# Two of a head pair's 32 row maxima taken by ScalarE and GpSimd, twelve value segments in place of thirteen, and the reciprocal of the row sums on VectorE

## The chip, the cores and the metric

The kernel runs on 1 core of one Trainium2 chip. The metric is the device time of one execution in microseconds (us), lower being better. A change of 0.2% is about 4.8 us here.

## The reference

One transformer layer with attention and a mixture of experts side by side, all in float32: x is 8 x 1024 x 256, 16 heads of 16, 8 experts of width 352 of which each token takes 2, and a shared expert of width 704.

```python
xn = _layernorm(x)
# attention, per batch row b and head h
Q, K, V = xn @ Wq + bq, xn @ Wk + bk, xn @ Wv + bv
scores = einsum('bqhd,bkhd->bhqk', Q, K) * 16 ** -0.5 + alibi
attn   = softmax(scores, axis=-1)                 # row max, exp, row sum
out    = einsum('bhqk,bkhd->bqhd', attn, V) @ Wo + bo
# experts
top_logits, idx = top_k(xf @ Wg, 2); probs = softmax(top_logits)
y = sum over the token's 2 experts of prob * (silu(xf@W1[e]) * (xf@W2[e])) @ W3[e]
y = y + (silu(xf@Ws1) * (xf@Ws2)) @ Ws3
return x + out + y
```

## The kernel before

One program order (`Order.run`) is walked by five classes (Tensor, Vector, Scalar, Pool, Sync), each of which issues its engine's part; `Turn.wait_ge` adds semaphore waits. So every engine executes in the order written there, and nothing reorders it.

The stages are: layer norm and projections (to about 200 us), attention (to about 1415 us), the 71 blocks of the routed experts (to about 1890 us), and the shared expert with the output projection.

Attention works on **pairs** of heads, 64 in all (`NPAIR`). For a pair r there are two passes over the 1024 x 1024 scores of each head:

- The **max pass** (`max_unit`, 32 units a pair): a matmul of 128 queries by 512 keys into one PSUM bank of a ring of four (banks 4 to 7), then VectorE reduces it to a row maximum in `mx`. A "double" (half-units 2k and 2k+1 where k stands in `DOUBLE`) is one reduction over two banks. After a pair's last unit `fold` (VectorE) takes the maximum of the two halves into `m16`, GpSimd negates it and splits it in high and low parts (`mneg`), VectorE transposes it (`max_rows`, `mT`), and SyncE sends it through HBM (`Md`) into rows 52 and 53 of the query operand (`place_rows`), so that the score matmul subtracts the maximum.
- The **score pass** (`scores`, 32 a pair): a matmul of 128 keys by 512 queries into a ring of three banks (0 to 2), then ScalarE's exp into one of eight `pt` buffers (`pta`, `ptb`). `values` multiplies those with V into bank 3, in four column groups at once; V holds 16 ones beside each head, so rows of bank 3 are the row sums.

The max pass runs ahead: when the score pass of pair r begins, the max pass stands at unit 24 of pair r+1.

`PAIR` writes the order out by hand, one string for two key chunks: `S` one score, `u` one max unit, `P` one value segment, `T` the transpose of the next pair's maxima. `WIDTHS` gives the columns of each `P`; a pair has 4096 of them (8 chunks of 512), and the segments run two chunks behind the scores. When a pair's last column is done ScalarE copies bank 3 to `accs`. `heads(r, i)` then turns the sums over: SyncE fetches them as 128 x 16 (`sq`), GpSimd raises them to the power -1 (i = 1), SyncE sends them out and back in broadcast (`Sd`, `asum`), GpSimd multiplies `accs` by them (i = 3), and SyncE stores the result.

Beside attention GpSimd also issues DMAs (clearing slots, packing expert weights, scattering rows, loading V), and in pairs 0 to 18 the routing (`route`, tiles `r_...`) runs in small steps on VectorE and GpSimd, two steps a pair.

In the profile the matmul line L569 is a helper's: all matmuls but the transposes have it. `ps<-OPS` with 54 or 52 rows are scores and max units, `ps<-pta,VB` and `ps<-ptb,VB` are value segments. L1054 is a double, L1051 a single reduction, L1064 the fold, L1070 the transpose, L889 the exp, L897 the copy of bank 3, L1314 to L1319 the negation, L1326 the power -1, L1330 the multiplication by it, L1581 and L1575 the two DMAs of the maxima.

## Time and profile before

| | us |
|---|---|
| time, median of 3 runs (2382.97 to 2386.32) | 2384.82 |
| span of the profiled execution, first to last instruction | 2353.9 |
| VectorE busy in the span | 1978.7 (84%) |
| TensorE busy | 2316.8 (98%) |
| ScalarE busy | 1709.7 (73%) |
| GpSimd busy | 1012.1 (43%) |

The profile gives no time of the profiled execution beyond its span; the median of the timed runs lies 30.9 us above it, which is start and end around the instructions. Shares of the whole span mix stages; in the slices of the page VectorE reads 9 (90% or more) in attention and 5 to 7 afterwards. TensorE's busy time is modelled at its matmuls' ends and pipelined, so 98% doesn't say that it has nothing to give. The granted TensorE clock was full in all 40 slices.

### The profile page before, as it was taken

How to read it: one execution, taken by the hardware profiler on the slowest of the kernel's cores; microseconds unless marked ns; L12 is line 12 of the kernel's file. 1: busy time of each engine (PE TensorE's matmuls, PEld its weight loads, DVE VectorE, ACT ScalarE, POOL GpSimd, SP SyncE). 2: the span in 40 equal slices, each digit the busy share in tenths (PEclk: the TensorE clock that was granted, in tenths of full speed). 3: DMA queues.
4: the chain of work that ended last, by engine and by line, in shares of the span. 5: the costliest groups of instructions: out<-in, count | busy, mean ns of one | idle time of the engine just before them, and what ended most of it. 6: DMA issues, size and time to landing. Idle time of an engine off the chain costs nothing.

```text
span 2353.9 us, 50539 instructions
## 1 busy us (share of the span) xinstructions
PE 2316.8 (98%) x19358; PEld 1543.2 (66%) x19358; DVE 1978.7 (84%) x2874; ACT 1709.7 (73%) x3276; POOL 1012.1 (43%) x1013
## 2 busy tenths in 40 slices
PE   7999999999999999999999999999999999999998
PEld 6875444444444444444444438999999989888998
DVE  7888999999999999999999966777777765555555
ACT  4447888888999999998999997777777753333332
POOL 2112556553225555454454334434343354455444
PEclk9999999999999999999999999999999999999999
DMA  8994544543224444343343335777777753344432
GB/s 295 375 338 173 169 155 161 165 145 99 81 83 131 125 123 136 114 128 118 121 127 109 108 96 192 241 240 236 242 236 247 233 174 108 108 129 125 123 108 90
DMA packets 189745, 383.07 MB, mean 163 GB/s; under 512 B 54164, under 2 KB 100756, under 8 KB 176292
## 3 DMA queue, kind: packets, MB, share of 16 engines
q1 hardware_dynamic: 151536, 219.17, 29.1%
q0 software_dynamic: 36880, 159.87, 21.3%
q8 instruction: 154, 2.52, 0.5%
q10 hardware_dynamic: 1088, 0.79, 0.1%
q14 instruction: 87, 0.71, 0.1%
HBM read 247.86 MB, written 140.31 MB: 165 GB/s over the span
## 4 chain that ended last, share of the span: by engine, by line
PE 65%; DVE 29%; issue 3%; ACT 2%; DMA 1%; SPq 0%; POOL 0%; DVEq 0%; POOLq 0%; ACTq 0%
PE ps L569 62%; DVE mx L1054 17%; DVE mx L1051 10%; PE ps L582 3%; DMA Md<-mT 1%; ACT ptb L889 0%; ACT pta L889 0%; ACT qkH L869 0%; DMA xr<-Xn 0%; DMA OPS<-Md 0%; DVE mT L1070 0%; SPq L1562 0%; DMA xt<-in_x 0%; DVE qkL L1041 0%; POOL rstd L1270 0%
## 5 line engine op out<-in xcount | busy, mean ns | idle before, releaser
L569 PE MATMUL ps<-OPS 54*128 54x512 f32 (+1 forms) x4096 | 734.7, 439 | 5.2 <-DMA OPS<-Md 2.4
L1054 DVE TENSOR_REDUCE mx<-ps 128x2 f32<-128x1024 f32 x620 | 734.2, 1216 | 5.7 <-PE ps L569 4.8
L569 PEld LDWEIGHTS ps<-OPS 54*128 54x128 f32 (+1 forms) x4096 | 366.3, 184 | 394.0 <-ACT pta L889 263.7
L889 ACT ACTIVATE pta<-ps 128x512 f32<-128x512 f32 x1024 | 549.7, 605 | 65.5 <-PE ps L569 56.8
L889 ACT ACTIVATE ptb<-ps 128x512 f32<-128x512 f32 x1024 | 544.9, 609 | 47.4 <-PE ps L569 38.8
L1051 DVE TENSOR_REDUCE mx<-ps 128x1 f32<-128x512 f32 x808 | 514.0, 677 | 2.1 <-PE ps L569 2.0
L569 PE MATMUL ps<-OPS,WB 128*128 128x256 f32 (+2 forms) x2364 | 384.5, 315 | 3.1 <-DVE VB L1181 1.5
L569 PEld LDWEIGHTS ps<-OPS,WB 128*128 128x128 f32 (+1 forms) x2364 | 332.3, 183 | 28.2 <-issue 3.9
L569 PE MATMUL ps<-pta,VB 128*32 128x192 f32 (+7 forms) x4520 | 324.7, 370 | 0.0
L569 PE MATMUL ps<-ptb,VB 128*32 128x512 f32 (+1 forms) x3064 | 296.9, 461 | 0.0
L1314 POOL TENSOR_SCALAR m<-m 128x16 f32<-128x16 f32 x64 | 16.9, 265 | 540.8 <-DVE m L1064 540.8
L569 PEld LDWEIGHTS ps<-pta,VB 128*32 128x32 f32 x4520 | 95.8, 108 | 174.1 <-issue 147.3
L569 PE MATMUL ps<-OPS,WB0c 128*128 128x256 f32 (+2 forms) x1248 | 206.4, 317 | 3.4 <-issue 2.6
L569 PE MATMUL ps<-WB,OPS 128*128 128x256 f32 (+1 forms) x1550 | 206.1, 283 | 0.0
L1326 POOL TENSOR_TENSOR sq<-sq,mone 128x16 f32<-128x16 f32 x64 | 194.1, 3032 | 3.7 <-DMA sq<-accs 3.1
L569 PEld LDWEIGHTS ps<-WB,OPS 128*128 128x128 f32 (+1 forms) x1550 | 194.8, 191 | 0.1
L569 PEld LDWEIGHTS ps<-OPS,WB0c 128*128 128x128 f32 (+1 forms) x1248 | 178.9, 183 | 19.6 <-issue 3.8
L1186 DVE TENSOR_TENSOR OPS<-VB,OPS 128x256 fp32r<-128x256 f32 (+1 forms) x213 | 150.3, 705 | 33.8 <-ACT OPS L937 33.8
L962 ACT ACTIVATE VB<-ps 128x512 f32<-128x512 f32 x80 | 47.6, 595 | 164.3 <-PE ps L569 163.9
L569 PEld LDWEIGHTS ps<-ptb,VB 128*32 128x32 f32 x3064 | 67.3, 108 | 136.1 <-issue 136.1
L1430 POOL DMA_INDIRECT Xs<-xr,slot x128 | 129.6, 1012 | 59.6 <-PE ps L569 50.9
L1486 POOL DMA_INDIRECT gath<-Ys,slot x128 | 130.4, 1019 | 36.5 <-issue 34.4
(172 smaller groups left out, 2867.5 us busy)
## 6 DMA issues: line engine op xcount, KB each, us to landing
OPS<-QKh SPq DMA_DIRECT2D x512, 64.0 KB
Xs<-zero POOLq DMA_DIRECT2D x71, 256.0 KB, 3.6
xr<-Xs SPq DMA_DIRECT2D x71, 256.0 KB, 5.3
Ys<-VB SPq DMA_DIRECT2D x71, 256.0 KB, 5.0
QKh<-qkH SPq DMA_DIRECT2D x16, 1024.0 KB, 7.3
QKl<-qkL SPq DMA_DIRECT2D x16, 1024.0 KB, 8.8
OPS<-QKl SPq DMA_DIRECT2D x256, 64.0 KB
asum<-Sd SPq DMA_DIRECT2D x64, 256.0 KB
```

The lines of the kernel that those rows point to most:

```text
L569: return self.e.matmul(o, l, r, start=start, stop=stop)
L582: return self.e.transpose(o, in_, ident[:, :])
L889: self.e.activation(pt(m)[:, half * GT:(half + 1) * GT], ps[:, score_bank(n), :], ACT.Exp).then_inc(sem["exp"], 1)
L962: self.e.activation(sg[:, k, :], ps[:, bank, :], ACT.Silu).then_inc(sem["sg"], 1)
L1051: self.e.reduce_max(mx[:, r % 2, hh, i, half:half + 1], ps[:, bank, :], AX.X).then_inc(sem["mxred"], 1)
L1054: self.e.reduce_max(mx[:, r % 2, hh, i, :], ps[:, bank - 1:bank + 1, :], AX.X).then_inc(sem["mxred"], 2)
L1186: e.tensor_tensor(HL[0:hn, s, 0:BT], hfq[0:hn, k, :], HH[0:hn, s, 0:BT].bitcast(F32), ALU.subtract).then_inc(sem["hl"], 1)
L1314: e.tensor_scalar(m16[:, k2, :, :], m16[:, k2, :, :], -1.0, None, ALU.mult).then_inc(sem["mng"], 1)
L1326: self.e.tensor_tensor(sq[:, :], sq[:, :], mone[:, :], ALU.pow).then_inc(sem["rcp"], 1)
L1430: e.indirect_dma_start(Xs[:, :], bass.IndirectOffsetOnAxis(ap=slot[:, c, 4 * g + j:4 * g + j + 1], axis=0), xr[:, k, j, :], None).then_inc ...
L1486: self.e.indirect_dma_start(gath[:, j, c, :], None, Ys[:, :], bass.IndirectOffsetOnAxis(ap=slot[:, c, i:i + 1], axis=0)).then_inc(sem[f"ga ...
```

## The change

1. Units 0 and 8 of every pair from pair 2 on (`COPIED`) are no longer reduced by VectorE. ScalarE copies the bank to SBUF (`mst`, a view of the weight buffer WB0 that is free during attention). After unit 8 GpSimd folds both 512-wide copies to 64 columns in three levels. Each level computes max(a - b, 0) + b with three instructions. VectorE takes the maximum over the 64 columns of both at once (`finish`, at unit 1 of the next pair).
2. `DOUBLE` goes from 10 doubles and 12 singles to 5 doubles and 20 singles a pair.
3. `fold` moves from unit 0 to unit 3 of the next pair (`FOLD_AT`), and GpSimd's negation from its place at unit 31 to unit 3.
4. `PAIR` and `WIDTHS`: 12 value segments a pair in place of 13, each string with three, their places moved forward by a score or more.
5. The power -1 of the row sums on GpSimd becomes a RECIPROCAL on VectorE at the same place of the program, except for the last pair.

```diff
 PAIR = (
-    "SuSuPSuSuPSuSuSuPSu",
-    "SuSuPSuSuPSuSuSuPSuT",
-    "SuSuPSuSuSuPSuSuSuP",
-    "SuSuPSuSuPSuSuPSuSuP",
+    "SuPSuSuSuPSuSuPSuSu",
+    "SuPSuSuSuPSuSuPSuSuT",
+    "SuPSuSuSuPSuSuPSuSu",
+    "SuPSuSuSuPSuSuPSuSu",
 )
-WIDTHS = 224, 288, 512, 288, 320, 512, 416, 512, 352, 160, 128, 192, 192
+WIDTHS = 416, 256, 352, 512, 256, 256, 416, 320, 288, 448, 288, 288
-DOUBLE = (0, 2, 5, 7, 8, 9, 10, 11, 12, 14)
+DOUBLE = (1, 5, 9, 13, 15)
+COPIED = (0, 8)
+FOLD_AT = 3
...
+            def max_unit(self, n, bank=None):                      # ScalarE
+                if not copied(n):
+                    return
...
+                self.w.wait_ge("mxmm", n + 1)
+                self.e.copy(mst[:, r % 2, COPIED.index(u), :], ps[:, ring.bank("max", n), :]).then_inc(sem["mxcp"], 1)
...
-                if u == 0 and r:
+                if u == 1 and r:
+                    self.finish(r - 1)
+                elif u == FOLD_AT and r:
                     self.fold(r - 1)
...
+            def finish(self, r):                                    # VectorE
...
+                self.w.wait_ge("mxl", 9 * (r - 1))
+                self.e.tensor_reduce(mx[:, r % 2, hh, i:last + 1:(last - i) // (NC - 1), side], mst[:, r % 2, :, 0:64],
+                                     AX.X, ALU.max).then_inc(sem["mxf"], 1)
...
+            def heads(self, r, i):                                  # VectorE
+                if i == 1 and r < NPAIR - 1:
+                    self.w.wait_ge("asd", 16 * (r + 1))
+                    self.e.reciprocal(sq[:, :], sq[:, :]).then_inc(sem["rcp"], 1)
...
+            def copied_max(self, n):                                # GpSimd
...
+                self.w.wait_ge("mxcp", copies(n) + 1)
+                done = 9 * (r - 2)
+                for level in range(3):
+                    half = 256 >> level
+                    a, b = m[:, :, 0:half], m[:, :, half:2 * half]
+                    self.w.wait_ge("mxl", done + 3 * level)
+                    e.tensor_tensor(a, a, b, ALU.subtract).then_inc(sem["mxl"], 1)
+                    self.w.wait_ge("mxl", done + 3 * level + 1)
+                    e.tensor_scalar(a, a, 0.0, None, ALU.max).then_inc(sem["mxl"], 1)
+                    self.w.wait_ge("mxl", done + 3 * level + 2)
+                    e.tensor_tensor(a, a, b, ALU.add).then_inc(sem["mxl"], 1)
...
             def heads(self, r, i):
-                if i == 1:
+                if i == 1 and r == NPAIR - 1:
```

The waits on `mxred` become waits on `mxred` or `mxcp` according to who frees the bank. What the tables do to TensorE's order in the middle of a pair, before (`OPS` rows are alternating scores and max units, so x6 is three of each; the last number of a value row is its four matmuls):

```order
L569 MATMUL ps<-pta,VB 32x352 x4
L569 MATMUL ps<-OPS 128x512 x4
L569 MATMUL ps<-pta,VB 32x160 x4
L569 MATMUL ps<-OPS 128x512 x4
L569 MATMUL ps<-pta,VB 32x128 x4
L569 MATMUL ps<-OPS 128x512 x4
L569 MATMUL ps<-pta,VB 32x192 x4
L569 MATMUL ps<-OPS 128x512 x4
L569 MATMUL ps<-pta,VB 32x192 x4
```

and now, around the units 0 to 8 of the next pair's maxima:

```order
L599 MATMUL ps<-OPS 128x512 x6
L599 MATMUL ps<-pta,VB 32x512 x4
L599 MATMUL ps<-OPS 128x512 x6
L599 MATMUL ps<-pta,VB 32x256 x4
L599 MATMUL ps<-OPS 128x512 x4
L599 MATMUL ps<-pta,VB 32x256 x4
L599 MATMUL ps<-OPS 128x512 x6
L599 MATMUL ps<-ptb,VB 32x416 x4
```

The short segments with two scores between them are gone; the first x6 above ends with the copied unit 0, and a segment of 512 columns stands behind it.

VectorE's order from one fold to beyond the transpose, before (units 0 to 9 of a pair):

```order
L1064 TENSOR_REDUCE m<-mx 128x16
L1054 TENSOR_REDUCE mx<-ps 128x2
L1051 TENSOR_REDUCE mx<-ps 128x1 x2
L1054 TENSOR_REDUCE mx<-ps 128x2
L1051 TENSOR_REDUCE mx<-ps 128x1 x2
L1070 STREAM_TRANSPOSE mT<-mneg 128x32
L1051 TENSOR_REDUCE mx<-ps 128x1 x2
```

and now (units 30 and 31, then 1 to 15; `WB` is where `mst` lies):

```order
L1095 TENSOR_REDUCE mx<-ps 128x2
L1092 TENSOR_REDUCE mx<-ps 128x1
L1111 TENSOR_REDUCE mx<-WB 128x2
L1095 TENSOR_REDUCE mx<-ps 128x2
L1119 TENSOR_REDUCE m<-mx 128x16
L1092 TENSOR_REDUCE mx<-ps 128x1 x4
L1125 STREAM_TRANSPOSE mT<-mneg 128x32
L1092 TENSOR_REDUCE mx<-ps 128x1
L1095 TENSOR_REDUCE mx<-ps 128x2
L1092 TENSOR_REDUCE mx<-ps 128x1 x4
L1131 RECIPROCAL sq<-sq 128x16
```

Units 0 and 8 are missing from VectorE's row, `finish` (L1111) and the reciprocal (L1131) are new in it, and only four single reductions lie between the fold and the transpose that needs GpSimd's negation of it.

## Rows read from the trace of the kernel before

**Rows 1.** The page: the chain of work that ended last, by line.

```profile
PE ps L569 62%; DVE mx L1054 17%; DVE mx L1051 10%; PE ps L582 3%; DMA Md<-mT 1%; ACT ptb L889 0%; ACT pta L889 0%; ACT qkH L869 0%; DMA xr<-Xn 0%; DMA OPS<-Md 0%; DVE mT L1070 0%; SPq L1562 0%; DMA xt<-in_x 0%; DVE qkL L1041 0%; POOL rstd L1270 0%
```

**Rows 2.** Windows: start:end, length, busy (count) of PE, PEld, DVE, ACT, POOL; clock, DMA.

```profile
220.00:554.00 334.00, 332.32 (x3140) 143.97 (x3136) 330.19 (x426) 296.32 (x567) 177.86 (x228) 1.00 0.49 154
554.00:1370.00 816.00, 815.00 (x7914) 351.29 (x7912) 812.63 (x1033) 742.30 (x1419) 367.63 (x382) 1.00 0.39 116
```

**Rows 3.** Groups of DVE in 220:554, count, busy, mean ns, idle before.

```profile
L1070 DVE STREAM_TRANSPOSE mT<-mneg 128x32 f32<-128x32 f32 x17 | 3.4, 199 | 0.0
```

**Rows 4.** Groups of DVE in 554:1370, columns as in rows 3.

```profile
L1054 DVE TENSOR_REDUCE mx<-ps 128x2 f32<-128x1024 f32 x431 | 509.9, 1217 | 1.9 <-PE ps L569 1.3 <-issue 0.2
...
L1064 DVE TENSOR_REDUCE m<-mx 128x16 f32<-128x32 f32 x43 | 8.0, 186 | 1.5
```

**Rows 5.** Timeline of DVE, fold to fold: start, length, instruction, xcount.

```profile
799.53 0.19 DVE L1064 TENSOR_REDUCE m<-mx 128x16 f32<-128x32 f32 x1
799.63 1.21 DVE L1054 TENSOR_REDUCE mx<-ps 128x2 f32<-128x1024 f32 x1
800.76 1.28 DVE L1051 TENSOR_REDUCE mx<-ps 128x1 f32<-128x512 f32 x2
801.96 1.21 DVE L1054 TENSOR_REDUCE mx<-ps 128x2 f32<-128x1024 f32 x1
...
804.28 0.20 DVE L1070 STREAM_TRANSPOSE mT<-mneg 128x32 f32<-128x32 f32 x1
...
818.44 0.19 DVE L1064 TENSOR_REDUCE m<-mx 128x16 f32<-128x32 f32 x1
```

**Rows 6.** Timeline of PE in the same pair.

```profile
799.70 0.73 PE L569 MATMUL ps<-OPS 54*128 54x512 f32 x4
800.36 0.75 PE L569 MATMUL ps<-pta,VB 128*32 128x224 f32 x16
801.04 0.97 PE L569 MATMUL ps<-OPS 54*128 54x512 f32 x6
801.94 0.91 PE L569 MATMUL ps<-pta,VB 128*32 128x416 f32 x8
...
810.01 0.43 PE L569 MATMUL ps<-pta,VB 128*32 128x128 f32 x8
810.37 0.77 PE L569 MATMUL ps<-OPS 54*128 54x512 f32 x4
```

**Rows 7.** Timeline of ACT in the same pair.

```profile
801.57 1.57 ACT L889 ACTIVATE ptb<-ps 128x512 f32<-128x512 f32 x3 [0.24 <-PE ps L569]
...
817.20 0.59 ACT L897 COPY accs<-ps 128x512 f32<-128x512 f32 x1
817.68 0.60 ACT L889 ACTIVATE pta<-ps 128x512 f32<-128x512 f32 x1
```

**Rows 8.** Groups of POOL and one of DVE over the whole span.

```profile
L1326 POOL TENSOR_TENSOR sq<-sq,mone 128x16 f32<-128x16 f32 x64 | 194.1, 3032 | 3.7 <-DMA sq<-accs 3.1
L1330 POOL TENSOR_TENSOR accs<-accs,asum 128x512 f32<-128x512 f32 x64 | 82.2, 1284 | 22.6 <-DMA asum<-Sd 22.6
L1296 POOL COPY VB<-vst 128x1024 f32<-128x1024 f32 x16 | 17.2, 1074 | 17.2 <-DMA vst<-Vd 17.2
L1113 DVE RECIPROCAL prob<-r_r 128x64 f32<-128x64 f32 x1 | 0.5, 543 | 0.0
```

**Rows 9.** Timeline of POOL: the negation and what follows it.

```profile
799.81 0.27 POOL L1314 TENSOR_SCALAR m<-m 128x16 f32<-128x16 f32 x1 [7.42 <-DVE m L1064]
...
800.49 0.23 POOL L1319 TENSOR_TENSOR mneg<-m,mneg 128x16 f32<-128x16 f32 x1
800.67 1.29 POOL L1330 TENSOR_TENSOR accs<-accs,asum 128x512 f32<-128x512 f32 x1
```

**Rows 10.** Chain of waits, 1043:1062, where the maxima came late.

```profile
1050.49 6.13 DMA Md<-mT
...
1056.92 2.83 DMA OPS<-Md
```

More of the change, by code:

```diff
@@ L71 @@
     "xt qkmm vmm mxmm smm pv obmm rtmm sct gmm up down sdn "
-    "wsplh woh xh qkh vev exp acc1 rte rtc wsh sch sg hh yev och "
-    "wspll bq wol ob st ag ve norm xl qkl mxred m16 mtr rcp rt rtw wslv scl hf hl ocl s1 gf fin "
-    "nhalf rstd lgc pad vcp ones zmem mng mnh mnl nrm rg rtd rtm rtp rtb rts wslp xb ya"
+    "mxcp wsplh woh xh qkh vev exp acc1 rte rtc wsh sch sg hh yev och "
+    "mxf wspll bq wol ob st ag ve norm xl qkl mxred m16 mtr rcp rt rtw wslv scl hf hl ocl s1 gf fin "
+    "mxl nhalf rstd lgc pad vcp ones zmem mng mnh mnl nrm rg rtd rtm rtp rtb rts wslp xb ya"
 ).split()
@@ L89, in score_bank, with copied, copies, reduced @@
     return n % 3 if tail < 0 else TAIL_BANKS[tail % 7]
+def copied(n):
+    return n >= 64 and n % 32 in COPIED
+def copies(n):
+    return 0 if n < 64 else (n - 64) // 32 * len(COPIED) + sum(u < n % 32 for u in COPIED)
+def reduced(n):
+    return n - copies(n)
 class Turn:
@@ L507, in build @@
         B.close()
+        mst = WB0[:, 2 * P:2 * P + 2 * NC * GT].bitcast(F32).rearrange("p (k s n) -> p k s n", k=2, s=NC)
         C = ExitStack()
@@ L555, in projections_over, with taken, maxima_over @@
                 w.wait_ge(f"xn{k}", 16 * len(range(k, NG, 3)))
+        def taken(w, n):
+            if copied(n):
+                w.wait_ge("mxcp", copies(n + 1))
+            else:
+                w.wait_ge("mxred", reduced(n + 1))
+        def maxima_over(w):
+            w.wait_ge("mxred", reduced(32 * NPAIR))
+            w.wait_ge("mxcp", copies(32 * NPAIR))
         def attention_over(w):
@@ L907, in route @@
                                     ).then_inc(sem["rtc"], 1)
+            def max_unit(self, n, bank=None):
+                if not copied(n):
+                    return
+                r, u = divmod(n, 32)
+                self.w.wait_ge("vmm", 4 * NG)
+                self.w.wait_ge("mxf", r - 3)
+                self.w.wait_ge("mxmm", n + 1)
+                self.e.copy(mst[:, r % 2, COPIED.index(u), :], ps[:, ring.bank("max", n), :]).then_inc(sem["mxcp"], 1)
             def split_block(self, b, i):
@@ L1048, in max_unit @@
                 bank = ring.bank("max", n) if bank is None else bank
-                if u // 2 not in DOUBLE or r < 2:
+                if copied(n):
+                    pass
+                elif u // 2 not in DOUBLE or r < 2:
                     self.w.wait_ge("mxmm", n + 1)
@@ L1054, in max_unit @@
                     self.e.reduce_max(mx[:, r % 2, hh, i, :], ps[:, bank - 1:bank + 1, :], AX.X).then_inc(sem["mxred"], 2)
-                if u == 0 and r:
+                if u == 1 and r:
+                    self.finish(r - 1)
+                elif u == FOLD_AT and r:
                     self.fold(r - 1)
                 elif n == 32 * NPAIR - 1:
+                    self.finish(r)
                     self.fold(r)
+            def finish(self, r):
+                if r < 2:
+                    return
+                hh, i, side = unit(32 * r + COPIED[0])[1:]
+                last = unit(32 * r + COPIED[-1])[2]
+                self.w.wait_ge("mxl", 9 * (r - 1))
+                self.e.tensor_reduce(mx[:, r % 2, hh, i:last + 1:(last - i) // (NC - 1), side], mst[:, r % 2, :, 0:64],
+                                     AX.X, ALU.max).then_inc(sem["mxf"], 1)
             def fold(self, r):
-                self.w.wait_ge("mxred", 32 * (r + 1))
+                self.w.wait_ge("mxred", reduced(32 * (r + 1)))
+                self.w.wait_ge("mxf", r - 1)
                 self.w.wait_ge("mnl", r - 1)
@@ L1308, in max_unit @@
             def max_unit(self, n, bank=None):
+                r, u = divmod(n, 32)
+                if copied(n):
+                    self.copied_max(n)
+                if u == FOLD_AT and r:
+                    self.negate(r - 1)
+                elif n == 32 * NPAIR - 1:
+                    self.negate(r)
+            def copied_max(self, n):
                 e = self.e
                 r, u = divmod(n, 32)
-                k2 = r % 2
-                if u == 31:
-                    self.w.wait_ge("m16", r + 1)
-                    e.tensor_scalar(m16[:, k2, :, :], m16[:, k2, :, :], -1.0, None, ALU.mult).then_inc(sem["mng"], 1)
-                    self.w.wait_ge("mtr", r - 1)
-                    self.w.wait_ge("mng", r + 1)
-                    e.tensor_copy(mneg[:, k2, :, 0, :].bitcast(F32R), m16[:, k2, :, :]).then_inc(sem["mnh"], 1)
-                    self.w.wait_ge("mnh", r + 1)
-                    e.tensor_tensor(mneg[:, k2, :, 1, :], m16[:, k2, :, :], mneg[:, k2, :, 0, :], ALU.subtract
-                                    ).then_inc(sem["mnl"], 1)
+                if u != COPIED[-1]:
+                    return
+                m = mst[:, r % 2, :, :]
+                self.w.wait_ge("mxcp", copies(n) + 1)
[9 more added lines that the diff above has]
+                    e.tensor_tensor(a, a, b, ALU.add).then_inc(sem["mxl"], 1)
@@ new lines, in negate @@
+            def negate(self, r):
+                e, k2 = self.e, r % 2
+                self.w.wait_ge("m16", r + 1)
+                e.tensor_scalar(m16[:, k2, :, :], m16[:, k2, :, :], -1.0, None, ALU.mult).then_inc(sem["mng"], 1)
+                self.w.wait_ge("mtr", r - 1)
+                self.w.wait_ge("mng", r + 1)
+                e.tensor_copy(mneg[:, k2, :, 0, :].bitcast(F32R), m16[:, k2, :, :]).then_inc(sem["mnh"], 1)
+                self.w.wait_ge("mnh", r + 1)
+                e.tensor_tensor(mneg[:, k2, :, 1, :], m16[:, k2, :, :], mneg[:, k2, :, 0, :], ALU.subtract
+                                ).then_inc(sem["mnl"], 1)
```

9 lines of the change are left out of this document (5 added, 4 removed).

## The prediction

> **What bounds the kernel now.** I read the chain of waits first: matmuls of L569 carry 62% of the end, and the two forms of row maximum on VectorE 27% [rows 1]. The row maxima exist only in attention, so that is the place to look. The windows over attention say the same of both halves of it: VectorE is busy 330.19 of 334 us while the routing steps run beside it and 812.63 of 816 us afterwards, TensorE 815.00 of 816, ScalarE 742.30, GpSimd 367.63, and the TensorE clock is granted in full [rows 2]. VectorE sat idle before its doubles for 1.9 us in 816 [rows 4]. So VectorE really is a bound. Whether TensorE is one too can't be seen from its busy time, since its matmuls' ends are modelled, and has to be built up from the starts of its groups (below).
>
> There are 43 folds, one a pair, in the second window, so a pair takes 816/43 = 18.98 us [rows 2, 4]; from fold to fold in the pair I use as a pattern it is 818.44 - 799.53 = 18.91 us [rows 5], and the difference of 0.07 us is the share of a few pairs that wait for late maxima, as the one whose first DMA took 6.13 us and whose second 2.83 us [rows 10]. In the first window there are 17 pairs in 334 us, 19.65 each [rows 2, 3]: the routing's steps on VectorE, 0.67 us a pair more. These 60 pairs are what the change acts on.
>
> **The change part by part, in us of one pair.**
>
> VectorE, by distances from start to start [rows 5]: a double 1.13 (799.63 to 800.76), a single 0.60 (two in 1.20, 800.76 to 801.96), the fold 0.10 (799.53 to 799.63). The transpose is as long in the rows as the fold (0.20 against 0.19), so 0.12. Before: 10 x 1.13 + 12 x 0.60 + 0.10 + 0.12 = 18.72, against 18.91 from fold to fold; the 0.19 that is left are small starts between kinds and the fold's own wait for the last maximum. After: 5 x 1.13 + 20 x 0.60 = 17.65, the fold and the transpose 0.22, and two new ones. `finish` reads 2 x 64 columns; it costs at least the fold (32 columns, 0.10) and at most a single (512 columns, 0.60), and in proportion between them 0.20, which I take. The reciprocal of 16 columns costs at least 0.10 too and at most the 0.54 that 64 columns take [rows 8]; a quarter of that is 0.14, and I take 0.15. Together 18.22, with bounds of 18.07 and 19.0; of the 0.19 about half stays, as the fold no longer stands behind the last maximum: 18.3. VectorE's own work falls by 0.6. Note that more singles is the dear part: a pair of units costs 1.20 as singles and 1.13 as a double, so 0.35 of the two units' 1.20 is given back.
>
> TensorE, again by starts [rows 6]. Scores and max units run side by side in two halves of the rows, and what costs is the change to a value segment and back: a group of two scores and two units takes 0.66 (799.70 to 800.36), one of three and three 0.90 (801.04 to 801.94). A value segment of 320 columns (224 + 96) takes 0.68 (800.36 to 801.04), one of 128 takes 0.36 (810.01 to 810.37); so 1.67 ns a column and 0.147 a segment. Before there are 13 segments, seven groups of two and six of three: 4.62 + 5.40 + 6.83 + 13 x 0.147 = 18.76. After, 12 segments, four groups of two and eight of three: 2.64 + 7.20 + 6.83 + 12 x 0.147 = 18.43. TensorE therefore stood only 0.15 below VectorE's 18.91, and it is the next bound: of VectorE's 0.6 at most 0.48 can be had, and with thirteen segments as before only 0.15 could.
>
> ScalarE: an exp repeats after (1.57 - 0.60)/2 = 0.485 and the copy of a bank after 0.48 (817.20 to 817.68) [rows 7]. Before 32 x 0.485 + 0.48 = 16.0, after 17.0 with two more copies. It has 1.4 to spare and nothing to add to the sum, but its idle time is in front of bursts: three banks of scores are all it is given. The copy stands behind an exp that waits for nearly the same matmul, and behind it comes a value segment of 512 or 416 columns (1.00 or 0.84), in which ScalarE may catch up. The cover is that segment; if it failed, two copies of 0.48 would show in TensorE's row, 1.0 a pair.
>
> GpSimd: the power of 3.03 goes, six two-input instructions come [rows 8]. One of 512 columns takes 1.28 and one of 16 takes 0.22 [rows 8, 9], so 256 take 0.74 and 128 take 0.46: 2 x (1.28 + 0.74 + 0.46) = 4.96. The three one-input maxima are shown nowhere at that width; half of the copy of 1024 columns (1.07) bounds them below, 1.3 for all three, the two-input price above, 2.5. Nine hand-overs of about 0.1 (799.81 + 0.27 to the second after it at 800.49, with one of 0.20 between [rows 9]) make 7.2 to 8.4. GpSimd goes from 367.63/43 = 8.5 to about 13.3 of 18.6 us [rows 2, 4]. None of it is on the path: the result is asked for 25 units later, some 14.5 us. The Trainium skill ("GPSIMD Engine Reference", section 4.1) puts one-input operations near line rate, which is the lower end, 7.2; the sum is the same by either.
>
> The fold, three units later, leaves four singles (2.4 us) before the transpose. GpSimd's negation ends 0.91 after its start and 1.2 after the fold's (799.53 to 800.49 + 0.23) [rows 5, 9]. It gets there in time if GpSimd is free, and it now comes to it having done its multiplication already; the transpose itself keeps its place, 16 scores before the pair that needs it, so the DMAs of the maxima have the half pair that they had, and the 0.07 of late ones stays.
>
> The added reciprocal makes VectorE wait for a DMA, and the next maximum is queued behind it. The fetch is issued just after the copy of bank 3 and has half a pair, 9 us; the power waited 3.1 us for it once in 64 [rows 8]. Nothing a pair.
>
> While GpSimd multiplies from 800.67 to 801.96, VectorE's two singles stand at the usual 1.20 [rows 5, 9]: maxima that read PSUM are not held up by it. The Trainium skill ("SBUF — State Buffer", section "Who interferes with whom") has a rule that speaks against more work on GpSimd: a VectorE instruction with two SBUF inputs and a GpSimd instruction that reads SBUF exclude each other for a whole instruction. By it the six routing steps of VectorE that read two tiles could each wait up to 1.28 us beside the new chain, 8 us at most, while the maxima, `finish` and the reciprocal read PSUM or one tile. No row here shows such a meeting, and the forecast is without it.
>
> **The sum.** Neither engine reaches its own figure, since VectorE (18.3) and TensorE (18.43) now run within 1% of each other with four banks between them. One gap can be followed. Units 30, 31 and 0 are a group of three (0.90), unit 0 is not VectorE's, and behind it TensorE spends 1.00 on a segment, so unit 1 starts 1.90 after unit 30; unit 31 starts a third of the group after it. A result is read 0.53 after its matmul's start (801.04 on TensorE to 801.57 on ScalarE [rows 6, 7]). VectorE has the double of 30 and 31 from 0.83 to 1.96 and unit 1 only at 2.43: up to 0.47 idle if it has no arrears, nothing if it is one unit late. I take half, 0.25: 18.55 a pair, 0.36 under 18.91. Over 43 pairs 15.5 us. In the 17 routing pairs VectorE is more clearly the bound and its arrears cover the gap; I take 0.5 of its 0.6: 8.5 us. Together 24 us: a span of 2330, and with the 30.9 us that lie between span and median, 2361 us. Before and after attention nothing of weight changes; once the maxima are over, ScalarE's exps bound the last pair and a half, as before.
>
> **Rivals.**
> 1. *Both floors are reached.* TensorE's 18.43 holds and VectorE's arrears hide every gap: 0.48 x 43 + 0.6 x 17 = 31 us, 2354; with the low ends of `finish` and the reciprocal and with steadier groups 38 us, 2347. For it: today TensorE and VectorE run at 18.76 and 18.91 at once with almost no idle. Against it: five doubles give fewer arrears than ten.
> 2. *Lock step.* Singles free banks one by one, the copy adds a third engine to the ring, and the pair settles at 18.85: 0.06 x 43 + 0.3 x 17 = 8 us, 2377. For it: VectorE's slack to TensorE is 0.13. Against it: the segments are now nearly even, where before a run of short ones met six doubles.
> 3. *Slower: GpSimd is late with the negation.* The transpose then stands on VectorE with all maxima behind it. From the copy of unit 8 to the negation there are 27 units, 16.0 us at today's pair of 18.98, with 1.2 of slack at the transpose, and GpSimd's other work takes 5.5 of it (8.5 a pair less the power's 3.0). So it decides from a chain of 11.7 us, where the pair is as long as today; each us beyond stretches the pair by 32/27, so at 12.2 it is 0.6 a pair, 36 us over 60 pairs, 2421. For it: the power takes 3.03 for 16 columns [rows 8], so GpSimd's price does not always go by width, and three one-input maxima of 2.5 would be enough. Against it: the small negation takes 0.27 [rows 9].
>
> **How the numbers follow.** The forecast, a pair at 18.45 to 18.75 and 2354 to 2372, has 0.69; rival 1 beyond that 0.12, rival 2 0.12, rival 3 0.07. The predicted time is 2361. The range runs from 2347 (the low ends of rival 1) to 2376 (most of rival 2), and leaves out rival 3 and the rest of rival 2. 0.2% is 4.8 us, about what this kernel's measurement can tell from no change: faster has the forecast, rival 1 and half of rival 2, 0.87; within 0.2% the other half, 0.06; slower 0.07.
>
> **What would show it.** From fold to fold 18.5 to 18.6; L1092 and L1095 with 20 and 5 a pair; VectorE with idle time before unit 1 that today's rows don't have; `finish` at 0.2 and the reciprocal at 0.15 from start to start; ScalarE's copy at 0.48; GpSimd's chain of nine under 9 us and the transpose waiting for nobody. Wrong would be a pair above 18.8, groups of scores on TensorE well over 0.66 and 0.90 that wait for ScalarE, or a transpose that waits for GpSimd.

## The result and the profile after

The changed kernel took 2391.16 us, median of 16 runs (2387.06 to 2398.49), the kernel before 2383.43 us beside it (16 runs, 2378.72 to 2388.25): ratio 1.0037 [1.0028, 1.0046]. It is slower by 0.4% (by the two medians alone 0.3%), and my 2361 us missed it on the wrong side. The profiled execution of the changed kernel took 2389.2 us with a span of 2387.4: 1.8 us lie around the span, where I had set 30.9.

The page's chain by line, after; it answers [rows 1]:

```profile
PE ps L599 87%; PE ps L612 3%; DVE mx L1092 2%; ACT pta L919 1%; DMA asum<-Sd 0%; DVE mx L1095 0%; ACT qkH L899 0%; ACT ptb L919 0%; DMA xr<-Xn 0%; DMA Sd<-sq 0%; SPq L1648 0%; DMA xt<-in_x 0%; DVE qkL L1080 0%; DMA Vd<-vs 0%; POOL rstd L1330 0%
```

VectorE's 27% fell to 2%, so by this chain its row maxima left the path, and TensorE's scores and value segments took it over. In windows of the same columns as [rows 2], the routing pairs, six ordinary pairs and the scatter stage of the changed kernel:

```profile
225.00:596.00 371.00, 365.07 (x3462) 160.62 (x3454) 358.04 (x562) 339.50 (x661) 281.48 (x390) 1.00 0.48 147
596.00:708.00 112.00, 112.00 (x1108) 47.80 (x1104) 109.73 (x175) 106.81 (x210) 61.30 (x82) 1.00 0.31 85
708.00:1344.00 636.00, 623.36 (x5934) 254.02 (x5926) 595.77 (x935) 575.84 (x1128) 469.47 (x577) 1.00 0.40 118
```

In the third window VectorE stands idle for 40 of 636 us and TensorE for 12.6, at full clock. So no engine is full here: they stand still together. What happens in one such pair, on GpSimd (timeline: start, length, instruction, idle time before it and what ended it):

```profile
845.59 1.11 POOL L1516 DMA_INDIRECT Xs<-xr,slot  x1 [0.15 <-issue]
846.99 0.98 POOL L1516 DMA_INDIRECT Xs<-xr,slot  x1 [0.30 <-issue]
```

and on ScalarE:

```profile
845.83 1.57 ACT L919 ACTIVATE pta<-ps 128x512 f32<-128x512 f32 x3 [0.22 <-PE ps L599]
848.45 1.09 ACT L919 ACTIVATE pta<-ps 128x512 f32<-128x512 f32 x2 [1.04 <-PE ps L599]
```

GpSimd issues two scatters (DMAs that place rows by an index) 1.40 us from start to start, right behind its chain of nine, and ScalarE then waits 1.04 us for TensorE. VectorE's next maximum stands at 848.43 with 0.54 idle. Such a wait stands in all 32 pairs of the scatter stage, in one of them 0.34 long, in the others 0.6 to 1.3, and these pairs last 19.28 to 19.99 us (28 of them 19.72 to 19.81; the starts of the copies of bank 3 mark the pairs) against 18.73 in the pairs without scatters.

**Where the time went.** Each pair copies its output sums once (`accs<-ps`), so the starts of these copies cut an execution into stretches. The first row is the execution that stood ahead of the prediction; "again" is a second execution of an unchanged kernel; the last is the best version found below. Holds are the 1-us waits just shown.

| us | to copy 0 | 0 to 19 (routing) | 19 to 24 | 24 to 57 (scatters) | to the end | span |
|---|---|---|---|---|---|---|
| before, no holds | 218.6 | 371.1 | 94.6 | 626.5 | 1042.9 | 2353.9 |
| before again, 23 holds | 219.6 | 371.3 | 94.6 | 647.6 | 1048.5 | 2381.6 |
| after, 32 holds | 223.8 | 375.2 | 93.6 | 651.2 | 1043.5 | 2387.4 |
| after again, no holds | 223.4 | 378.5 | 93.7 | 619.6 | 1041.7 | 2357.0 |
| best version, no holds | 218.8 | 371.6 | 93.7 | 618.5 | 1041.5 | 2344.1 |

Three things are to be read from it. An ordinary pair went from 18.92 to 18.73 (94.6/5, 93.6/5), half of my 0.36. The setup and the routing pairs lost 8 to 12 us where I had forecast a gain of 8.5. And 28 us in before, 30 in the changed kernel, lie between two executions of one and the same kernel.

### The profile page after: what moved, and what is told of

It reads as the page before. It is cut to its first block, busy times and chain, and to the rows that moved or that the text cites. A ratio compares the mean times of both kernels' runs of the same rounds, so it can differ in the third digit from the quotient of the medians.

```text
span 2387.4 us, 51358 instructions
## 1 busy us (share of the span) xinstructions
PE 2332.1 (98%) x19366; PEld 1536.1 (64%) x19366; DVE 1951.8 (82%) x3185; ACT 1750.3 (73%) x3400; POOL 1316.5 (55%) x1508
## 4 chain that ended last, share of the span: by engine, by line
PE 90%; DVE 4%; ACT 2%; DMA 1%; issue 1%; POOL 1%; SPq 0%; DVEq 0%; POOLq 0%; ACTq 0%
PE ps L599 87%; PE ps L612 3%; DVE mx L1092 2%; ACT pta L919 1%; DMA asum<-Sd 0%; DVE mx L1095 0%; ACT qkH L899 0%; ACT ptb L919 0%; DMA xr<-Xn 0%; DMA Sd<-sq 0%; SPq L1648 0%; DMA xt<-in_x 0%; DVE qkL L1080 0%; DMA Vd<-vs 0%; POOL rstd L1330 0%
## 5 line engine op out<-in xcount | busy, mean ns | idle before, releaser
L1092 DVE TENSOR_REDUCE mx<-ps 128x1 f32<-128x512 f32 x1304 | 817.7, 679 | 56.9 <-PE ps L599 54.5
L599 PE MATMUL ps<-OPS 54*128 54x512 f32 (+1 forms) x4096 | 750.7, 445 | 24.3 <-ACT pta L919 13.1
L919 ACT ACTIVATE ptb<-ps 128x512 f32<-128x512 f32 x1024 | 555.6, 631 | 35.1 <-PE ps L599 18.3
L1095 DVE TENSOR_REDUCE mx<-ps 128x2 f32<-128x1024 f32 x310 | 376.8, 1215 | 5.1 <-PE ps L599 3.8
L599 PE MATMUL ps<-ptb,VB 128*32 128x416 f32 (+3 forms) x4048 | 300.6, 392 | 0.0
L599 PE MATMUL ps<-pta,VB 128*32 128x288 f32 (+2 forms) x3544 | 299.6, 424 | 0.0
L1392 POOL TENSOR_SCALAR WB<-WB 128x512 f32<-128x512 f32 x186 | 177.9, 956 | 16.5
L1390 POOL TENSOR_TENSOR WB<-WB 128x512 f32<-128x512 f32 x186 | 155.1, 834 | 45.5 <-ACT WB L946 35.0
L1394 POOL TENSOR_TENSOR WB<-WB 128x512 f32<-128x512 f32 x186 | 153.2, 824 | 15.5
L1416 POOL TENSOR_TENSOR accs<-accs,asum 128x512 f32<-128x512 f32 x64 | 82.3, 1286 | 134.0 <-DMA asum<-Sd 133.7
L599 PEld LDWEIGHTS ps<-ptb,VB 128*32 128x32 f32 x4048 | 81.5, 108 | 104.0 <-issue 103.9
```

What stands on the lines that cost most here:

```text
L599: return self.e.matmul(o, l, r, start=start, stop=stop)
L919: self.e.activation(pt(m)[:, half * GT:(half + 1) * GT], ps[:, score_bank(n), :], ACT.Exp).then_inc(sem["exp"], 1)
L1092: self.e.reduce_max(mx[:, r % 2, hh, i, half:half + 1], ps[:, bank, :], AX.X).then_inc(sem["mxred"], 1)
L1095: self.e.reduce_max(mx[:, r % 2, hh, i, :], ps[:, bank - 1:bank + 1, :], AX.X).then_inc(sem["mxred"], 2)
L1390: e.tensor_tensor(a, a, b, ALU.subtract).then_inc(sem["mxl"], 1)
L1392: e.tensor_scalar(a, a, 0.0, None, ALU.max).then_inc(sem["mxl"], 1)
```

## The experiments

Theory A, formed from the two traces: two indirect scatters back to back make TensorE's results reach the others 1 us late. The rivals are named in the expectations.

**before_again.** No edit.

> The kernel before, unchanged, for a second profiled execution. Open question: its recorded execution spans 2353.9 us, while its timed runs lie at 2379 to 2388, and in the profile of the changed kernel the time is only 1.8 us above the span. Theory C (before's ordinary execution holds stalls that its recorded one does not show): a span near 2380, with some pairs of the scatter stage at 19.7 instead of 18.9 us. If theory C is wrong: a span near 2354 again, all pairs of the stage at 18.9, and the time 2 us above the span.

2383.37 us, span 2381.6. Theory C holds: the execution that I had predicted from had none of the holds that this one, as long as the timed runs, has. In one profile before has pairs of both kinds. GpSimd and ScalarE in a held pair, then in one that isn't:

```profile
844.94 1.05 POOL L1430 DMA_INDIRECT Xs<-xr,slot  x1 [0.16 <-PE ps L569]
846.30 0.96 POOL L1430 DMA_INDIRECT Xs<-xr,slot  x1 [0.31 <-issue]
...
847.01 0.60 ACT L889 ACTIVATE ptb<-ps 128x512 f32<-128x512 f32 x1 [1.04 <-PE ps L569]
...
884.68 1.05 POOL L1430 DMA_INDIRECT Xs<-xr,slot  x1 [0.16 <-PE ps L569]
885.75 0.61 POOL L1289 DMA_DIRECT2D vst<-Vd  x1
886.66 1.01 POOL L1430 DMA_INDIRECT Xs<-xr,slot  x1 [0.30 <-PE ps L569]
...
886.04 0.60 ACT L889 ACTIVATE ptb<-ps 128x512 f32<-128x512 f32 x1 [0.33 <-PE ps L569]
```

Of 24 pairs with the two 1.4 us apart 23 are held (19.5 to 20.2 us), of 8 with 2.0 us none (18.91 to 19.11). The one of the 24 that isn't held is also the only one whose two scatters stand 5.0 us behind the copy, the others standing 3.8 to 3.9 behind it, so the place in the pair may count as well as the distance. The scatter stage accounts for 21.0 of the 27.7 us between the two profiles. Another 5.5 lie behind copy 57, where nothing is scattered; I did not follow them.

**e1_before_chain.** Before, plus in each pair from the third:

```
+ if u == 8 and r >= 2:
+     self.w.wait_ge("mxmm", n + 1)
+     self.chain(r)      # subtract, max 0, add at 256, 128 and 64 columns, on an unused buffer
```

> The kernel before with GpSimd's nine-step chain alone, on a buffer that nobody reads or writes (so no ScalarE copies, no changed order, no finish step, reciprocal still on GpSimd). Theory A (the chain pushes the two late indirect scatters of a pair back to back, and while both are under way TensorE's semaphore updates come 1 us late): pairs of the scatter stage rise from 18.9 to 19.7 or 19.9, 33 pairs, +27 to +34 us, and the routing steps that VectorE runs beside the chain take 1.9 and 3.4 us in place of 0.3, +5 us or so. Theory B (the delay comes with the changed order or the ScalarE copies, not with the chain): within 5 us of before, pairs at 18.9.

2638.48 us, ratio 1.1073 [1.1048, 1.1097]: far above either expectation, so it tells nothing on the scatters. What it shows, in the waits of 740:1600 (sum, times, longest):

```profile
POOL accs L1349 <- DMA asum<-Sd: 165.3, 34, 8.9
```

Here the power of 2.94 us stands behind the chain in GpSimd's queue, so the sums' round trip begins late, and then GpSimd itself stands still for its return; pairs take 18.9 to 29 us. e14 takes up which of the two, the chain or the power behind it, costs this.

**e2_after_split.** The chain in two pieces, in the pairs with scatters:

```
+ self.levels(r, m, done, (0,) if r >= SCAT_AT + 2 and r < NPAIR - 4 else range(3))
...
+ if kc == 5:
+     self.chain_rest(r + 2)     # levels 1 and 2, behind the scatter of key chunk 5
```

> The changed kernel, where in the scatter stage (pairs 28 to 59) level 0 of the chain (three instructions) runs before, and levels 1 and 2 (six instructions) after, the scatter of key chunk 5; nothing else differs. So some 4 us of GpSimd's work stand between the two late scatters. Theory A: the hold of 1.05 us a pair goes, pairs of the stage 18.7 instead of 19.75, about 33 us less, near 2358. Theory B: GpSimd does the same work, the same copies and order remain, so the pairs stay at 19.75 and the time at 2391.

2358.84 us where before takes 2384.55, ratio 0.9899 [0.9877, 0.9920]; the scatter stage takes 619.6 instead of 651.2 us. Theory A holds, B fails: the same work in another order on GpSimd is worth 32 us. (On the same chip e3, which leaves the chain whole, takes 31 us more.)

**e3_after_exp.** `self.w.wait_ge("exp", n)` in place of `"smm"` in `scatter_rows`.

> The changed kernel, with the scatters waiting for ScalarE's exponential of the unit instead of TensorE's matmul of it (the semaphore that GpSimd waits on is another one; the place in the program is the same). After the chain GpSimd is late, so both late scatters would still issue back to back. Theory A: no change, pairs at 19.75, 2391 us. Rival B2 (it is GpSimd's wait on the semaphore that TensorE counts up which holds TensorE's updates): the hold goes, pairs at 18.7, near 2358.

2389.77 us, ratio 1.0020 [1.0008, 1.0032], pairs at 19.6 to 20.0: which semaphore GpSimd waits on doesn't matter.

**e4_before_apart, e5_after_pack, e6_after_all, e7_after_dose** ran on another chip.

```
e4, e8:      + if n % 32 == 12: e.memset(pause[:, :], 0.0)          # 128x512, before kc 3's scatter
e5 (on e2):  - ... and kc == 1: self.pack_expert(r // 2)
             + ... and kc == 3: self.pack_expert(r // 2)
e6 (on e5):  VectorE's routing steps 30 and 31 become 37 and 39
e7, e9, e11, e15:
             + if n % 32 == 28 and n // 32 % 4:
             +     e.memset(pause[:, 0:(0, 128, 256, 512)[n // 32 % 4]], 0.0)
```

> The kernel before, plus one memset of an unused 128x512 buffer on GpSimd between the scatters of key chunks 1 and 3 in each pair of the scatter stage (no other change). In the second profile of before those two stand 1.36 us apart in 22 of its 32 pairs (19.5 to 20.2 us each) and 1.98 us apart in the others (18.9 to 19.1). The memset puts about 0.6 us between them. Theory A: all pairs at 18.92, 22 x 1.0 to 1.2 us less, 2384 - 25 = 2357 to 2360. Theory B (the delay has to do with something else in these pairs): unchanged at 2384, or slower by the memsets.

2360.55 us, but before took 2360.06 here as well: ratio 1.0005 [0.9996, 1.0014]. The expectation came true for no reason of its own.

> The changed kernel, with a memset on GpSimd between the two late scatters in three of every four pairs: none, 128x128, 128x256 and 128x512 in turn (about 0, 0.25, 0.35 and 0.6 us more between them, that is 1.38, 1.65, 1.75 and 2.0 us from start to start). Theory A with the bound that the second profile of before suggests (1.36 us held, 1.98 us not): the pairs without memset stay at 19.75, those with the longest are at 18.75, and the middle ones show where the bound lies. Theory B: all pairs stay at 19.75. One look, by the pairs' periods.

2358.14 us, all pairs of the stage at 18.7 to 19.0, those with 1.4 us between the scatters too. So this chip doesn't hold at all, whatever the spacing. The hold hangs on the spacing and on something that goes with the chip. Each chip was used in one session only, so whether it is the chip itself or a state that it was in isn't shown; "a chip that holds" stands for both.

> The changed kernel with the split chain (2358.8 us), and the five weight-packing DMA issues of even pairs moved from behind key chunk 1 to behind key chunk 3, so that on GpSimd they stand behind the negation and no longer ahead of it. Theory D (the change moved the negation behind these issues and behind those of the setup; VectorE's transpose then waits 4.5 us for it in pair 0 and about 1 us in each of seven others): the first of the late-maxima stalls falls from 3.7 us to near 0, the time by 5 to 9 us, 2350 to 2354. Rival: the later pack and the chain that now starts behind it cost GpSimd the same time elsewhere (the chain ends later, finish waits): 2359 or more.

2359.07 us, ratio 0.9997 [0.9987, 1.0006], where e2 took 2358.84: the 5 to 9 us don't come. The profiled execution, the fastest of the ten (2351.8 us), does reach copy 0 at 220.3 instead of e2's 224.8 us. The expectation also counted too many waits: up to copy 19 the changed kernel has three transposes that wait for the negation, 4.49, 0.97 and 1.30 us.

> As the one before, and VectorE's two routing steps that took 1.89 and 3.43 us beside GpSimd's work (0.30 and 0.25 in the kernel before) moved to the ends of pairs 18 and 19, where GpSimd has no 128x512 routing step. Theory E (each lasts until GpSimd's instruction beside it ends, and costs the pair of 24.2 us about 5): 4 to 5 us less again, 2345 to 2349. Rival (the pair is long because GpSimd's queue is late, whatever VectorE does): unchanged.

2347.36 us, ratio 0.9952 [0.9938, 0.9966], 11.7 us under e5 where I had expected 4 to 5. What the moved steps did in the changed kernel, on VectorE and, beside them, on GpSimd:

```profile
504.57 1.89 DVE L1195 TENSOR_SCALAR bex<-bex 128x71 f32<-128x71 f32 x1
...
515.32 3.43 DVE L1199 TENSOR_SCALAR widx<-bex,crow 128x71 int32<-128x71 f32 x1
```

```profile
503.77 1.39 POOL L1470 TENSOR_TENSOR r_pb<-r_pa,r_eq 128x512 f32<-128x512 f32 x1
505.01 1.39 POOL L1390 TENSOR_TENSOR WB<-WB 128x512 f32<-128x512 f32 x1
...
515.95 1.53 POOL L1473 TENSOR_TENSOR r_pb<-r_pb,r_first 128x512 f32<-128x512 f32 x1
517.18 1.51 POOL L1416 TENSOR_TENSOR accs<-accs,asum 128x512 f32<-128x512 f32 x1
```

They end with GpSimd's instructions, at 506.46 (505.01 + 1.39 = 506.40) and 518.75 (517.18 + 1.51 = 518.69). In e6 they take 0.19 and 0.90 us:

```profile
L1202 DVE TENSOR_SCALAR widx<-bex,crow 128x71 int32<-128x71 f32 x1 | 0.9, 899 | 0.0
L1198 DVE TENSOR_SCALAR bex<-bex 128x71 f32<-128x71 f32 x1 | 0.2, 186 | 0.0
```

In e5 they took 1.89 and 2.23, so their move gives back 3 us by itself. Most of the rest goes with the clock. The same window in `after_again` and in e6 (columns of [rows 2]):

```profile
470.00:530.00 60.00, 55.56 (x469) 23.53 (x468) 53.44 (x76) 46.46 (x91) 38.70 (x55) 0.89 0.40 127
```

```profile
470.00:530.00 60.00, 59.96 (x580) 26.01 (x572) 58.84 (x94) 56.25 (x111) 48.91 (x69) 1.00 0.47 144
```

In `after_again` TensorE is granted 0.89 of full speed over these 60 us, in e6 all of it. It has 1.2 GHz in two stretches of 6.8 us. The one from 520.4 on begins at the end of the second of the routing steps (517.54 + 3.43 = 520.97); the one from 486.3 on stands ahead of both, behind a transpose that waited for the negation until 484.55, and that is what e5 moved. In e5's profile only the one behind the steps is left, 3.4 us from 516.2 on (0.97 over the window). Over the timed runs the mean clock is 0.994 in e5 and 0.997 in e6, and 0.003 of 2350 us is 7 us. That is an estimate from the means: no profile of a typical e5 run shows the seven.

**The same again, for the other kind of chip.** Four kernels unchanged, on a third chip.

> The changed kernel, unchanged, on whichever chip it falls. So far the kernel before took 2382 to 2389 us where its neighbouring scatters (1.36 us apart) are followed by a hold, and 2360.06 on another chip, where neither it nor the changed kernel with memsets (pairs 18.72 throughout, also those without a memset) shows one. Theory F (the change's verdict hangs on whether the chip holds): where before takes 2360, the changed kernel takes 2356 to 2360 (no holds, 33 x 1.05 less than 2391); where before takes 2384, it takes 2391 again. Rival: it stays 7 us behind before on both.

2359.13 us where before takes 2360.74: ratio 0.9988 [0.9978, 0.9999]. On such a chip the change is a gain of 0.1%, hardly clear of nothing. GpSimd and ScalarE in a pair of it:

```profile
861.81 1.05 POOL L1516 DMA_INDIRECT Xs<-xr,slot  x1 [0.16 <-issue]
863.16 0.98 POOL L1516 DMA_INDIRECT Xs<-xr,slot  x1 [0.30 <-issue]
...
862.10 2.62 ACT L919 ACTIVATE pta<-ps 128x512 f32<-128x512 f32 x5 [0.23 <-PE ps L599]
```

The scatters stand 1.35 us apart, and five exps run without the pause that cut them into three and two on the holding chip.

> The kernel before with the 128x512 memset between the scatters of key chunks 1 and 3, again. On a chip where before takes 2384: theory A says 2357 to 2362 (scatters 1.78 us or more apart, no holds); the rival B says 2384. On a chip where before takes 2360 it shows nothing new: 2360.

2362.92 us, ratio 1.0004 [0.9994, 1.0014]: nothing new.

> The changed kernel with memsets of four lengths in turn (none, 128x128, 128x256, 128x512) between the two late scatters, again. On a chip where before takes 2384: theory A says pairs at 19.75 without memset and 18.75 with the longest, and the middle ones show the bound; rival B says all at 19.75. On the other kind of chip: all at 18.72.

2360.96 us, no pair held. The next two texts are the same question again: e11 on a fourth chip (before 2359.01) gave 2354.97 and e15 on a fifth (before 2360.61) 2357.90, the same reading.

> The changed kernel with memsets of four lengths in turn (none, 128x128, 128x256, 128x512) between the two late scatters, for a chip on which before takes 2380 or more. Theory A there: pairs at 19.75 without memset, 18.75 with the longest, the middle ones show the bound; rival B: all at 19.75. Where before takes 2360: all at 18.72, as twice before.

> The changed kernel with memsets of four lengths in turn (none, 128x128, 128x256, 128x512) between the two late scatters, again for a chip on which before takes 2380 or more; three chips so far were of the other kind (before at 2359 to 2361, all pairs at 18.72). On a holding chip theory A says 19.75 without memset and 18.75 with the longest; rival B all at 19.75.

> The changed kernel with split chain, weight packing behind the negation and the two routing steps moved (2347.4 us where before took 2360.1). Its late scatters stand over 3 us apart, so theory A says 2347 to 2350 on either kind of chip; if other things are held on a chip where before takes 2384, it is 2370 or more there.

2347.88 us, ratio 0.9944 [0.9926, 0.9961]: e6 confirmed, again on a chip that doesn't hold.

**e12_before_order** takes only the changed pair strings and the twelve widths over into before.

> The kernel before with the changed kernel's order (the pair's strings) and twelve value segments instead of thirteen; all 32 maxima on VectorE, reciprocal on GpSimd. My reading (VectorE's 18.9 us of maxima set the pair in before): pairs stay at 18.9 to 19.0, since VectorE's work is the same; within 3 us of before, where no scatters are held. Rival (TensorE's floor sets the pair: one segment start less, 0.33 us a pair): pairs of 18.6 to 18.7, 10 us or more less.

2492.66 us, ratio 1.0570 [1.0552, 1.0587], pairs of 21.31. Both expectations fail, by 2.4 us a pair. In its waits of 600:1300:

```profile
DVE mx L1054 <- PE ps L569: 64.9, 118, 1.1
```

My reading, which no run tests further, is that before's ten doubles fall on places where the new order has only one of the two banks filled. The order is no part that can be had alone, and how much of the 0.19 is its own stays open.

**e13_before_reciprocal** takes only the reciprocal over (`heads` of VectorE as in the change).

> The kernel before with the reciprocal of the row sums on VectorE, not on GpSimd (as in the changed kernel, all but the last pair's); nothing else. My term (0.15 us of VectorE a pair, which is full in this kernel): pairs from 18.92 to 19.07, 60 pairs, +8 us where no scatters are held. Rival (VectorE waits here for the round trip of the sums, since the order has other places): 19.3 or more, +20. Rival (hidden in VectorE's small idle): no change.

2358.54 us, ratio 1.0000 [0.9990, 1.0011], pairs of 18.94. Of its 0.16 us a pair 0.02 are to be seen, so 0.14 found room: VectorE was not full at 18.91.

**e14_all_pow** is e6 with the reciprocal back on GpSimd.

> The version of 2347.4 us (split chain, packing behind the negation, routing steps moved) with the reciprocal back on GpSimd as a power, behind the chain in its queue. Before plus the chain took 2638 with the power in its queue. Theory G (it is the power behind the chain that makes GpSimd late: the sums' round trip starts late, and GpSimd then waits for its own transfer): pairs of 20 to 28 us again, 2550 or more. Rival (the order and copies matter, GpSimd has 16.3 of 18.7 us of work with the power and room for it): 18.6 to 18.8 a pair, 2340 to 2350.

2536.18 us (one run). Theory G holds. The power in GpSimd's row, and what is waited for in 740:1300:

```profile
909.97 2.93 POOL L1423 TENSOR_TENSOR sq<-sq,mone 128x16 f32<-128x16 f32 x1
```

```profile
POOL accs L1427 <- DMA asum<-Sd: 53.8, 12, 8.6
...
DVE mT L1128 <- POOL mneg L1416: 36.7, 15, 4.8
```

So the power [rows 8] behind the chain costs some 189 us (2536.2 - 2347.4), and the reciprocal's move, which alone brings nothing (e13), is what makes the chain bearable at all.

**e16_after_routing** is the changed kernel with the memsets of e7 and, of e6, only the two routing steps moved.

> The changed kernel, of whose parts only VectorE's two routing steps are moved to the ends of pairs 18 and 19 (chain unsplit, weight packing ahead of the negation as in the change), and with the memsets of four lengths between the late scatters in turn. Moving these steps on top of the other edits gave 11.7 us (2359.07 to 2347.36), twice the 4 to 5 that I had expected. On a chip where before takes 2360: if the routing steps alone cost that much, 2347 to 2349; if a part of it is paid only once the negation is on time too, 2351 to 2356. On a chip where before takes 2384: pairs at 19.75 without memset and 18.75 with the longest (theory A), so about 8 x 1.05 us more than on the other kind.

It fell on a second chip that holds (before 2384.19 us): 2369.16 us, ratio 0.9944 [0.9927, 0.9960]. Within one execution, a pair with 128x256 columns of memset (GpSimd, then ScalarE), and one with 128x128:

```profile
956.17 1.10 POOL L1520 DMA_INDIRECT Xs<-xr,slot  x1 [0.16 <-issue]
957.26 0.35 POOL L1518 MEMSET WB<- 128x256 f32 x1
957.77 0.98 POOL L1520 DMA_INDIRECT Xs<-xr,slot  x1 [0.17 <-issue]
...
956.45 2.63 ACT L921 ACTIVATE pta<-ps 128x512 f32<-128x512 f32 x5 [0.23 <-PE ps L601]
```

```profile
1013.48 1.05 POOL L1520 DMA_INDIRECT Xs<-xr,slot  x1 [0.15 <-issue]
1014.53 0.23 POOL L1518 MEMSET WB<- 128x128 f32 x1
1014.93 0.98 POOL L1520 DMA_INDIRECT Xs<-xr,slot  x1 [0.17 <-issue]
...
1016.40 1.09 ACT L921 ACTIVATE pta<-ps 128x512 f32<-128x512 f32 x2 [1.05 <-PE ps L601]
```

| start to start | pairs | held | median pair |
|---|---|---|---|
| 1.36 to 1.46 us | 16 | 16 | 19.81 |
| 1.60 to 1.62 us | 8 | 1 | 18.73 |
| 1.75 to 1.78 us | 8 | 0 | 18.73 |

For these two scatters the bound lies between 1.46 and 1.60 us, and 0.15 us on GpSimd decide over 1.05 us of the engines that wait for TensorE. Without its 16 or 17 holds this kernel would take about 2369.2 - 17.3 = 2352 us, against 2359 for the change on a chip that doesn't hold. By this estimate, which sets two chips side by side, the routing steps alone are worth some 7 of the 11.7 us.

## Why the prediction was wrong

I had forecast 24 us less; between the profile of before again and that of the changed kernel, both with holds, it is 5.8 us more. Some 10 of these 30 us are holds that the chain added, 12 the routing pairs (a loss of 3.9 for a gain of 8.5), 4 the setup, and 6 to 7 the ordinary pairs (9 us saved for 15.5). That makes 33; about 4 come back behind copy 57, where before again was slow for a cause that I did not follow.

**The chain is covered.** This step failed: "None of it is on the path." At 8.5 us (662.46 to 670.96) it lay just above my 7.2 to 8.4, and its result was never waited for: no `finish` has idle time before it. But it is a queue, and I had only asked who waits for its end:

```profile
662.46 1.28 POOL L1390 TENSOR_TENSOR WB<-WB 128x512 f32<-128x512 f32 x1 [1.87 <-ACT WB L946]
663.83 1.49 POOL L1392 TENSOR_SCALAR WB<-WB 128x512 f32<-128x512 f32 x1
...
670.50 0.46 POOL L1394 TENSOR_TENSOR WB<-WB 128x128 f32<-128x128 f32 x1
```

Of the 8.5 us, the scatter of key chunk 5 spends the last part ready and queued; it goes out behind the chain, 1.4 us before key chunk 7's. In before the power stood at another place, and the pair of neighbours was chunks 1 and 3, back to back in 24 of 32 pairs. On a holding chip the change made that 32 of 32. The stage takes 651.2 - 647.6 = 3.6 us more than before, though its 33 pairs are 0.19 shorter by themselves (6.3 us): the holds that the change added cost some 10 us. My lower end by one-input operations "near line rate" (the Trainium skill, "GPSIMD Engine Reference", section 4.1) was wrong here: the one-input step of 512 columns took 1.49 us, more than the two-input one's 1.28.

**GpSimd is free for the negation.** "GpSimd gets there in time if it is free": it isn't in those even pairs that pack weights, where by its place behind unit 3 it now stands after the five DMA issues of the packing, and in pair 0 behind the setup's too. On GpSimd, then VectorE:

```profile
204.89 0.76 POOL L1499 DMA_DIRECT2D Xs<-zero  x1
205.53 0.42 POOL L1400 TENSOR_SCALAR m<-m 128x16 f32<-128x16 f32 x1
```

```profile
206.56 0.21 DVE L1125 STREAM_TRANSPOSE mT<-mneg 128x32 f32<-128x32 f32 x1 [4.49 <-POOL mneg L1405]
```

In before one transpose of 64 waits for the negation, the last, 1.0 us. This one cost TensorE 3.7 us, and in 200:226 the granted clock is 0.80 (1.00 and 0.93 in the two profiles of before), 10 us of it at 1.2 GHz. Copy 0 comes 4 to 5 us later. It is rival 3's mechanism, at places where I had not looked for it: not the chain's length decided, but what the negation was moved past. With the power back behind the chain (e14) it came in many pairs.

**The routing pairs gain 8.5 us.** They lost 4 to 7. The Trainium skill ("SBUF — State Buffer", section "Who interferes with whom") had it in the same section whose two-input rule I weighed: `tensor_scalar` can contend with GpSimd too. My half sentence on what reads PSUM or one tile had passed over VectorE's one-input routing steps. The trace agrees: 1.89 and 3.43 us against 0.30 and 0.25 in before. One of the two-input meetings that I had priced and left out came as well. In the changed kernel this step stands beside GpSimd's copy of V (279.55 to 280.86), which in before had ended 1.6 us ahead of it, and takes 2.26 us where it took 0.68:

```profile
279.15 2.26 DVE L1162 TENSOR_TENSOR r_eq<-r_pa,r_m 128x512 f32<-128x512 f32 x1
```

Together the three steps are 6.4 us longer. No run moved this one, and it is still 2.27 in e6, whose routing pairs take 371.6 us and so gain nothing on before either. The maxima that read PSUM stood at 0.60 throughout, as I had said.

**The pair at 18.55.** It came to 18.73, near the upper end of the forecast's 18.45 to 18.75. The terms of VectorE's own work were right: 20 and 5 reductions a pair, `finish` 0.19 from start to start (658.10 to 658.29 below), the reciprocal 0.16 (510.50 to 510.66), the copy 0.47 (657.14 to 657.61). The reciprocal waits for its DMA once, 14.6 us at 1438.6, when the last maximum has long been taken. VectorE in the changed kernel has the gap before unit 1 that I had followed:

```profile
655.90 1.22 DVE L1095 TENSOR_REDUCE mx<-ps 128x2 f32<-128x1024 f32 x1
657.49 0.69 DVE L1092 TENSOR_REDUCE mx<-ps 128x1 f32<-128x512 f32 x1 [0.37 <-PE ps L599]
658.10 0.28 DVE L1111 TENSOR_REDUCE mx<-WB 128x2 f32<-128x128 f32 x1
658.29 1.22 DVE L1095 TENSOR_REDUCE mx<-ps 128x2 f32<-128x1024 f32 x1
```

What failed is the term "I take half, 0.25". From the start of the double to that of unit 1 it is 1.59 us where a double takes 1.13, so the gap is 0.46, all of the 0.47 that I had worked out for a VectorE without arrears; in the five ordinary pairs behind copy 19 it is the same. With it the sum gives 18.76. I had also taken VectorE's 18.91 for a bound, and e13 shows 0.14 of it to have been slack. TensorE's group of two scores and two units next to it takes 0.83 instead of 0.66, so its floor of 18.43 isn't reached either:

```profile
658.40 0.91 PE L599 MATMUL ps<-OPS 54*128 54x512 f32 x4
659.23 0.64 PE L599 MATMUL ps<-pta,VB 128*32 128x256 f32 x8
```

That is lock step, rival 2, by half. Over the pairs from copy 19 on, where nothing is held, it saves 9 us (94.6 - 93.7, 626.5 - 619.6, 1042.9 - 1041.7), against my 15.5.

**From span to median, 30.9 us.** This was no gap around the instructions, which is 1.8 us. As far as the records show it was a span of one kind of chip set against a median of the other; on which chip the first profile was taken they don't say, but it has no hold. Before takes some 24 us less where nothing is held (2359 to 2361 against 2383 to 2384). The other 4 to 5 us are that the profiled execution, about 2355.7 us long, was faster than the median of its own kind. Had I known, the forecast for a chip like the profile's would have been 2332 from the profile, or 2336 from that kind's median, where 2359 was measured; that the latter lies near my 2361 is chance.

## What to carry to other kernels

When work is added to a queue, ask what it delays there and what will then leave it back to back, not only who waits for the result. When a step moves, list every instruction and DMA issue it is moved past, pair by pair, also the rare ones. A span and a median that lie 1% apart are two different executions; get the second profile before building a sum on the first.
